# Decoder layer on one core: weights loaded in halves on two queues, chunk 1's query and key projections ahead of chunk 0's transposes

## Time and profile before

| | |
|---|---|
| median of three runs (lowest to highest) | 863.43 us (862.97 to 863.92) |
| the profiled execution, its span | 862.34 us, 860.5 us |
| PE busy | 749.3 us (87%) |
| DVE busy | 544.0 us (63%) |
| ACT busy | 321.1 us (37%) |
| POOL busy | 129.4 us (15%) |
| granted clock of TensorE, mean | 0.936 |
| DMA, mean | 48 GB/s |

### The profile page before, as it was taken

One profiled execution on the slowest core, in us unless ns is written; L12 is line 12 of the kernel. 1 busy time (PEld: TensorE's weight loads), 2 busy tenths in 40 slices (PEclk: granted clock), 3 DMA queues, 4 the chain that ended last, 5 costly groups with the idle time before them and its releaser, 6 DMA issues.

```text
span 860.5 us, 12175 instructions
## 1 busy us (share of the span) xinstructions
PE 749.3 (87%) x4742; PEld 612.8 (71%) x4742; DVE 544.0 (63%) x1032; ACT 321.1 (37%) x559; POOL 129.4 (15%) x173
## 2 busy tenths in 40 slices
PE   4799988887998799525999999999999999899993
PEld 3688777766877587414888777886768877688882
DVE  3567578775667758769771847855578746542214
ACT  4232232225422432157443335353443544341312
POOL 0452334023322233044000000000000000000000
PEclk9899999997998899655999999999999999999997
DMA  8400100013100130040102012002111030010201
GB/s 306 171 26 1 38 13 13 1 26 123 32 7 1 38 99 1 1 147 1 50 1 74 0 50 98 1 25 98 48 53 45 0 122 1 1 50 0 98 1 49
DMA packets 25356, 41.11 MB, mean 48 GB/s; under 512 B 4954, under 2 KB 7642, under 8 KB 25178
## 3 DMA queue, kind: packets, MB, share of 16 engines
q1 hardware_dynamic: 23194, 37.27, 12.9%
q10 hardware_dynamic: 2112, 3.15, 1.1%
HBM read 28.88 MB, written 11.53 MB: 47 GB/s over the span
## 4 chain that ended last, share of the span: by engine, by line
PE 39%; DVE 8%; ACT 2%; issue 2%; DVEq 0%; ACTq 0%
PE ps L1460 24%; PE ps L1470 11%; PE ps L457 2%; DVE act_s L279 2%; PE ps L468 2%; DVE act_s L376 1%; DVE silu L1393 1%; ACT silu L1330 1%; PE ps L477 1%; DVE xc L1406 1%; ACT h_hi L1313 1%; DVE xb L406 1%; DVE e_stats L409 1%; PE ps L450 1%; DVE w L279 0%
## 5 line engine op out<-in xcount | busy, mean ns | idle before, releaser
L1460 PE MATMUL ps<-x2T_lo,wgu_hi 128*128 128x512 f32 x352 | 141.1, 401 | 0.8 <-DVE x2T_lo L1383 0.8
L1460 PE MATMUL ps<-x2T_hi,wgu_lo 128*128 128x512 f32 x352 | 137.3, 390 | 0.0
L1460 PE MATMUL ps<-x2T_hi,wgu_hi 128*128 128x512 f32 x352 | 137.2, 390 | 0.0
L1393 DVE TENSOR_TENSOR silu<-ps,silu 128x512 f32<-128x512 f32 x44 | 30.4, 690 | 100.2 <-PE ps L1460 99.9
L1045 PE MATMUL ps<-wqkv_lo,xT_hi 128*128 128x512 f32 x192 | 83.0, 433 | 10.5 <-DVE masked L972 6.2
L1045 PE MATMUL ps<-wqkv_hi,xT_lo 128*128 128x512 f32 x192 | 78.4, 408 | 0.0
L1045 PE MATMUL ps<-wqkv_hi,xT_hi 128*128 128x512 f32 x192 | 78.2, 407 | 0.0
L1460 PEld LDWEIGHTS ps<-x2T_lo,wgu_hi 128*128 128x128 f32 x352 | 66.2, 188 | 15.3 <-DVE x2T_lo L1383 1.5
L1460 PEld LDWEIGHTS ps<-x2T_hi,wgu_lo 128*128 128x128 f32 x352 | 66.1, 188 | 14.0
L1460 PEld LDWEIGHTS ps<-x2T_hi,wgu_hi 128*128 128x128 f32 x352 | 66.2, 188 | 12.9
L1470 PE MATMUL ps<-wdn_lo,h_hi 128*128 128x512 f32 x176 | 70.6, 401 | 3.7 <-DVE h_lo L1377 3.7
(11 more groups left out here) (170 smaller groups left out, 1473.8 us busy)
## 6 DMA issues: line engine op xcount, KB each, us to landing
x_in<-in_x_dram SPq DMA_DIRECT2D x16, 256.0 KB, 3.5
w<-in_fside_BxS2xS_dram SPq DMA_DIRECT2D x4, 1024.0 KB, 6.5
x_dram<-xb SPq DMA_DIRECT2D x4, 1024.0 KB, 5.1
xc<-x_dram SPq DMA_DIRECT2D x4, 1024.0 KB, 5.4
xb<-x_dram SPq DMA_DIRECT2D x3, 1024.0 KB, 5.4
out_dram<-xc SPq DMA_DIRECT2D x3, 1024.0 KB, 4.2
z<-in_x_dram SPq DMA_DIRECT2D x3, 768.0 KB, 4.7
x_dram<-z SPq DMA_DIRECT2D x3, 768.0 KB, 4.0
```

The source lines that it names most:

```text
L1393: nc.vector.tensor_tensor(silu[:, it % 2, :], ps[5][:, :], silu[:, it % 2, :], ALU.mult)\
L1460: last = nc.tensor.matmul(dst[:, :], lhs, rhs, start=(k == 0 and n == 0), stop=(k == NK - 1 and n == 2))
```

## The change

The loads of Wq, Wk and Wv are each cut in two halves of 512 KB, the first on SyncE's queue, the second on ScalarE's, with a semaphore for each half. The identity matrix and x of chunk 1 move to ScalarE's queue; the tables, the mask and the scales follow in another order on SyncE's. On TensorE the transposes of x1 stand between q0 and k0; behind v0 come q1, the scale matmuls and k1, and then chunk 0's transposes. `weight_hi(3)` moves in ScalarE's list behind the copies of q1 and k1, and TensorE's waits for the scale columns and for Wo move to just ahead of the first y. `x_hi(1)` and `x_lo(1)` move ahead of Wv's rounding. In chunks 1 to 14 nothing changes.

```diff
@@ -537,9 +537,12 @@
 
 def attention_order():
 
-    yield from (("xT", 0), ("q", 0), ("k", 0), ("xT", 1), ("v", 0))
+    yield from (("xT", 0), ("q", 0), ("xT", 1), ("k", 0), ("v", 0), ("q", 1), ("k", 1))
     for n in range(CHUNKS):
-        yield from (("qT", n), ("kT", n), ("q", n + 1), ("k", n + 1), ("s0", n), ("s1", n), ("s2", n), ("s3", n))
+        yield from (("qT", n), ("kT", n))
+        if n > 0:
+            yield from (("q", n + 1), ("k", n + 1))
+        yield from (("s0", n), ("s1", n), ("s2", n), ("s3", n))
         if n % NC < NC - 1:
             yield ("kv", n)
         yield from (("v", n + 1), ("attn", n), ("xT", n + 2), ("y", n), ("ss", n))
@@ -613,7 +616,7 @@
         scale_rows = sq_halves[:, 0:2 * P].rearrange("p (m n) -> p m n", m=2)
         ident16 = sq_halves[:, 2 * P:3 * P]
 
-        tab_in, mask_in, wqkv_in, wo_in = (sem("tab_in"), sem("mask_in"), [sem(f"w{n}_in") for n in "qkv"],
+        tab_in, mask_in, wqkv_in, wo_in = (sem("tab_in"), sem("mask_in"), [[sem(f"w{n}_in_{m}") for m in range(2)] for n in "qkv"],
                                            sem("wo_in"))
         x_loaded = [sem("x_even_loaded"), sem("x_odd_loaded")]
         z_first_loaded, z_loaded = sem("z_first_loaded"), sem("z_loaded")
@@ -673,6 +676,11 @@
             for name, place in EXPERT0_STEPS.items():
                 if place == (n, part) and name in steps:
                     steps[name](0)
+
+        def load_half(eng, n, weight, half):
+
+            ks = slice(half * KH, (half + 1) * KH)
+            eng.dma_start(raw[:, n, ks], weight.rearrange("(k p) n -> p k n", p=P)[:, ks]).then_inc(wqkv_in[n][half], 16)
 
         gu_words = a["L0_ffn_gate_up_packed"].rearrange("(t p) w -> p t w", p=P).bitcast(U16)
         dn_words = a["L0_ffn_down_packed"].rearrange("(t p) w -> p t w", p=P).bitcast(U16)
@@ -723,15 +731,14 @@
                     sp.dma_start(dst, src).then_inc(words_in, 16)
 
             load_x(0)
-            sp.dma_start(ident_ones[:, :, :], table[:, 0:2 * P].rearrange("p (m n) -> p m n", m=2))\
-                .then_inc(ident_in, 16)
-            sp.dma_start(raw[:, 1], w_k.rearrange("(k p) n -> p k n", p=P)).then_inc(wqkv_in[1], 16)
+            load_half(sp, 0, w_q, 0)
+            load_half(sp, 1, w_k, 0)
+            sp.dma_start(tab[:, :], table[:, 2 * P:TABLE_W]).then_inc(tab_in, 16)
+            load_half(sp, 2, w_v, 0)
+            sp.dma_start(mask[:, :, :, :], masks.rearrange("p (j g c) -> p j g c", j=HG, g=NG)).then_inc(mask_in, 16)
             gu_rows, dn_rows = scale_rows[0:SCALES[0], 0, :], scale_rows[0:SCALES[1], 1, :]
             sp.dma_start(gu_rows, a["L0_ffn_gate_up_scales"].rearrange("g (t p) -> (g t) p", p=P)).then_inc(scales_in, 16)
             sp.dma_start(dn_rows, a["L0_ffn_down_scales"].rearrange("g (t p) -> (g t) p", p=P)).then_inc(scales_in, 16)
-            sp.dma_start(tab[:, :], table[:, 2 * P:TABLE_W]).then_inc(tab_in, 16)
-            load_x(1)
-            sp.dma_start(mask[:, :, :, :], masks.rearrange("p (j g c) -> p j g c", j=HG, g=NG)).then_inc(mask_in, 16)
             load_words(0)
             sp.wait_ge(w_ready, 4 * NK)
             load_z(0, True)
@@ -765,8 +772,12 @@
         @block.scalar
         def _(act):
             steps = expert.scalar_steps(act)
-            act.dma_start(raw[:, 0], w_q.rearrange("(k p) n -> p k n", p=P)).then_inc(wqkv_in[0], 16)
-            act.dma_start(raw[:, 2], w_v.rearrange("(k p) n -> p k n", p=P)).then_inc(wqkv_in[2], 16)
+            act.dma_start(ident_ones[:, :, :], table[:, 0:2 * P].rearrange("p (m n) -> p m n", m=2))\
+                .then_inc(ident_in, 16)
+            load_half(act, 0, w_q, 1)
+            load_half(act, 1, w_k, 1)
+            act.dma_start(x_in[:, 1, :], x_v[0][:, 1, :]).then_inc(x_loaded[1], 16)
+            load_half(act, 2, w_v, 1)
             act.dma_start(raw[:, 3], w_o.rearrange("(k p) n -> p k n", p=P)).then_inc(wo_in, 16)
             act.dma_start(rms_col[:, :], rms_w.rearrange("(k p) -> p k", p=P), allow_slow_non_contiguous=True)\
                 .then_inc(wo_in, 16)
@@ -774,7 +785,7 @@
             def weight_hi(n):
                 for k in range(NK):
                     if n < 3:
-                        act.wait_ge(wqkv_in[n], 16)
+                        act.wait_ge(wqkv_in[n][k // KH], 16)
                     else:
                         act.wait_ge(wo_scaled, k + 1)
                     dst = wqkv_hi[:, n, k, :] if n < 3 else wo_hi[:, k, :]
@@ -803,13 +814,17 @@
 
             def chunk(n):
                 b, c = divmod(n, NC)
+                if n == 0:
+                    projected(1, 0)
+                    projected(1, 1)
+                    weight_hi(3)
                 wait_full(act, "kT", n)
                 nc.scalar.activation(kT_hi[:, :, :], in_groups("kT", n), ACT.Copy).then_inc(kT_hi_done, 1)
                 wait_full(act, "qT", n)
                 nc.scalar.activation(qT_hi[:, :, :], in_groups("qT", n), ACT.Copy).then_inc(qT_hi_done, 1)
                 if c == 0 and b > 0:
                     ln_root_of(b - 1)
-                if n + 1 < CHUNKS:
+                if 0 < n < CHUNKS - 1:
                     projected(n + 1, 0)
                     projected(n + 1, 1)
                 beside(steps, n, 0)
@@ -833,11 +848,10 @@
             weight_hi(0)
             weight_hi(1)
             projected(0, 0)
+            x_hi(1)
             weight_hi(2)
             projected(0, 1)
-            x_hi(1)
             projected(0, 2)
-            weight_hi(3)
             act.wait_ge(ident_in, 16)
             nc.scalar.activation(ident16, ident, ACT.Copy).then_inc(ident16_set, 1)
             act.wait_ge(scale_ps, 2)
@@ -996,8 +1010,8 @@
             x_lo(0)
             weight_lo(0)
             weight_lo(1)
+            x_lo(1)
             weight_lo(2)
-            x_lo(1)
             dve.wait_ge(wo_in, 32)
             for k in range(NK):
                 nc.vector.tensor_scalar(raw[:, 3, k, :], raw[:, 3, k, :], rms_col[:, k:k + 1], None,
@@ -1047,8 +1061,21 @@
                 if ks[-1] == NK - 1:
                     last.then_inc(full[BANK_OF[u]], 1)
 
+            def scale_columns():
+                pe.wait_ge(ident16_set, 1)
+                pe.wait_ge(scales_in, 32)
+                at = 0
+                for m, n in enumerate(SCALES):
+                    nc.tensor.matmul(ps[6][:, at:at + n], scale_rows[0:n, m, :], ident16[0:n, 0:n],
+                                     start=True, stop=True).then_inc(scale_ps, 1)
+                    at += n
+
             def chunk(n):
                 c = n % NC
+                if n == 0:
+                    project(1, 0)
+                    scale_columns()
+                    project(1, 1)
                 pe.wait_ge(rot_done, 2 * (n + 1))
                 for p, u in enumerate(("qT", "kT")):
                     filled = start_use(u, n)
@@ -1103,6 +1130,9 @@
                     project(n + 1, 2, range(NK // 2, NK))
                 if n + 2 < CHUNKS:
                     transpose_x(n + 2)
+                if n == 0:
+                    pe.wait_ge(cols_set, 1)
+                    pe.wait_ge(w_ready, 4 * NK)
                 pe.wait_ge(o_lo_done, n + 1)
                 filled = start_use("y", n)
                 for k in range(NK):
@@ -1122,17 +1152,8 @@
             for p in range(3):
                 pe.wait_ge(w_ready, (p + 1) * NK)
                 project(0, p)
-                if p == 1:
+                if p == 0:
                     transpose_x(1)
-            pe.wait_ge(ident16_set, 1)
-            pe.wait_ge(scales_in, 32)
-            at = 0
-            for m, n in enumerate(SCALES):
-                nc.tensor.matmul(ps[6][:, at:at + n], scale_rows[0:n, m, :], ident16[0:n, 0:n],
-                                 start=True, stop=True).then_inc(scale_ps, 1)
-                at += n
-            pe.wait_ge(cols_set, 1)
-            pe.wait_ge(w_ready, 4 * NK)
             for n in range(CHUNKS):
                 chunk(n)
 
```

## The result

The changed kernel takes 867.14 us (median of 7, 865.45 to 868.25) against 863.92 (861.89 to 864.71) of the kernel before, run beside it: ratio 1.0036, 95% interval 1.0025 to 1.0046. It is slower by 3.2 us. The profiled execution has a span of 863.7 against 860.5.

The account below looks back on a forecast made before the run. TensorE's exit from the first 50 us was taken to bound the kernel, a shift there arriving nearly whole. Late x2 +1.5 and slow clock +1.7 gave +3.2 on the median 863.43: 866.6 us, range 862.6 to 868.5.

Parts of the forecast that it names:

- rival A: Chunk 0: x2 late, but the clock holds or a later fall vanishes in exchange; +0.5 to +2.2, 864.9 us; chance 0.2.
- Loads, q0, k0, v0, q1, k1: Front before chunk 0's transposes: q0 starts at 10.8 instead of 12.58, v0 at 20.0 instead of 21.16, k1 done at 28.5.
- rival C: Front loads: Wq's halves land no earlier than 9.29, q0 starts at 12.6 as now; +5.0, 868.4 us; chance 0.08.
- the bound I had named: q0 on TensorE: in the bounding case all of it runs slow, taking 0.4 us more.
- Wo's rounding: ScalarE, then VectorE: rounding starts at 29.1 instead of 24.72, subtraction takes 3.4, Wo ready at 33.2 (bounds 32.2 and 33.9).
- Chunk 0, "I charge 1.2": Scores to v1's first half at 1.2 GHz until about 39, partly covered by the masks' 3.0 us; cost 1.2 us.
- x2's load: SyncE: lands 12.8 us after Wo is ready, so x2's transposes start at 46.0 instead of 44.50, +1.5 (+0.5 to +2.2).
- Clock after the stall, +1.7: After 3.6 us idle before x2's transposes, y0, chunk 1's transposes and part of q2 run at 1.2 GHz; +1.7 us.
- The granted clock of one half between 45 and 51: TensorE around x2's transposes: a stretch at half clock there was named as a sign that the forecast is right.
- Passing through: From 50 us to the kernel's end: a shift at 50 us should arrive nearly whole at the end.
- Rival D: Past 100 us: VectorE-bound chunks take up the shift at 50 us; 863.4 to 864.5 us; chance 0.11.
- Rival B: Chunk 0: Wo's rounding not late, x2 in time, early scores count in full; -2.1, 861.3 us; chance 0.09.

Follow-up runs that it names:

- e8: Changed kernel with 24 idle-filling matmuls ahead of chunk 0's scores and x of chunk 2 loaded before SyncE's wait for Wo; ratio to the kernel before 0.9970.
- e7: Changed kernel with 24 idle-filling matmuls on TensorE between chunk 0's transposes and its scores; ratio to the kernel before 1.0043.
- e1: Changed kernel with x of chunk 2 loaded before SyncE's wait for Wo; ratio to the kernel before 1.0029.
- e11: Kernel before with 13 useless matmuls on TensorE just ahead of x2's transposes in chunk 0; ratio to the kernel before 1.0040.
- e2: Changed kernel with Wo rounded on ScalarE right behind the copy of v0 and the small identity; ratio to the kernel before 0.9975.
- e12: Changed kernel with Wo rounded behind v0's copy, chunk 2's x loaded before the wait for Wo, k1 back behind chunk 0's transposes; 855.44 us, ratio 0.9914.
- e10: Changed kernel with Wo rounded behind v0's copy, ten filling matmuls ahead of chunk 0's scores, chunk 2's x loaded before the wait for Wo; ratio 0.9948.
- e3: Changed kernel with Wo rounded behind v0's copy and x of chunk 2 loaded before the wait for Wo; ratio to the kernel before 0.9995.

## Why the prediction was right, and where its sum was not

The time (+3.2 forecast, +3.2 measured), its sign and the root of the loss, Wo's late rounding, were right. That the size agrees to a tenth is luck: two terms missed in opposite directions. x2's transposes came 2.83 later, not 1.5 and beyond the bound of 2.2; the clock after the wait cost nothing, not 1.7. In kind this is my rival A (x2 late, the clock holds), with a later x2 than I gave it. The 1.7 itself was half of a stretch of 3.3, where the row that I took it from gives 3.6.

- *Loads, q0, k0, v0, q1, k1.* q0 10.39 (forecast 10.8), v0 20.38 (20.0), chunk 0's transposes 29.14 (28.5). I had the rounding begin when Wq lands, at 7.5. It began at 7.10, straight behind x_hi(0) at 6.61, as before the change at 9.29 behind x_hi(0) at 8.80: there TensorE's first transposes had waited for the identity until 7.64. After, x_hi(0) follows a table load of ScalarE (5.31 to 6.59), and this its seven DMA issues, three more than before, which I had costed at nothing. The first half of Wq had landed at 1.18 + 5.5 = 6.7. So q0's gain came through the identity, and rival C, which hangs q0 on Wq's landing, misses this wait; what the halves alone gave, no run shows. All of q0 ran at 1.2 GHz, the bound I had named.
- *Wo's rounding.* Right in kind: ScalarE starts it at 29.83 (29.1). The subtraction was mis-sized: 4.25 instead of 3.4, above even the 3.71 of the row it was taken from, in which GpSimd worked beside it only part of the way. Wo ready at 34.7 (33.2, upper bound 33.9), scores at 36.14 (34.5).
- *Chunk 0, "I charge 1.2".* This term failed. From scores to TensorE ready for x2 takes 46.15 - 36.14 = 10.0 after, 6.7 in e8 with the clock held: 3.3 us. I had the clock return 4.4 us after work resumed, as in the rows of before; it took 7.4 (36.14 to 43.6). And the step "so part of it is covered" was wrong: the scores, which stand ahead of the masks, slow down too, and the slow first half of v1 ends at 43.5, later than the masks (41.4). Alone it cost nothing on the path, since x2 landed only at 47.3 (e7); it decides once x2 is early (x2's transposes at 46.10 in e1, at 41.80 in e8, whose front is 1.2 sooner).
- *x2's load.* 47.33 - 34.73 = 12.6 after Wo ready, forecast 12.8. x2 is what TensorE waits for, at 47.3 instead of 46.0; but TensorE came later too, so the wait was 1.18, not 3.6.
- *Clock after the stall, +1.7.* It did not happen: the clock held over the wait of 1.18. e7, where the wait was 3.19, shows that mechanism with its fall at 44.5 and return at 48. The granted clock of one half between 45 and 51, which I had named as a sign of being right, is not there in the changed kernel.
- *Passing through.* Right: 2.88 at chunk 1, 2.98 at chunk 8, 3.2 in the span, and e11. In 12 of the 13 kernels set against the one before, the spans differ by what chunk 8 did, to within 0.5 us (e8: 1.3). Rival D is out. Rival B's condition (Wo ready by 31.7) is what e2 made true, and it gave the gain.
- The Trainium skill (TensorE: Matmul & The Clock Gate, Part 1) has the release of the clock fall elsewhere from run to run. Here the runs agree, with one execution of each kernel: over the ten kernels with the changed loads and x1's transposes ahead of k0, v0 starts 8.8 us (e8: 19.29 - 10.53) to 10.2 us (e12: 20.48 - 10.32) behind q0, with the same work between.

What stays open: why the clock fell behind chunk 4 in some kernels and not in others. The single profiled executions move against the kernel before by up to 4.4 us between chunks 4 and 8 (e1: from +1.6 to +6.0), and no run fixed it. So the whole times, other than chunk 1, also hold this part, and they rank the kernels less surely than the front does.

## What to carry to other kernels

When work is moved ahead in one engine's list, look at what the other engines' lists put behind it: here two projections moved forward on TensorE pushed Wo's rounding behind their copies on ScalarE, and a semaphore that gated 3 MB of loads with it. Price idle time of TensorE with the slow stretch that follows it, and fill it with real work rather than shorten it. Remove coupled waits together, since one alone may show little.

## What the runs showed of the hardware

- The clock fell over an idle time of 2.27 us (e2) and held over one of 2.45 at 209 us (before). At 115.5, before, it fell right behind one of 1.94. The slow stretch in e2 lasted 6.8 us (32.0 to 38.8), the one in the changed kernel, with 5.96 us of idle time, 10.2 (33.3 to 43.6), and the one in e7, over the wait of 3.19, 3.4 (44.5 to 47.9).
- VectorE's subtraction of two SBUF operands took 4.25 us beside GpSimd's products and 2.50 without; GpSimd's four products took 4.11 beside it, and 2.76 in e2, where VectorE's work beside them had an operand in PSUM (kT_lo and qT_lo, 0.69 and 0.68, for 1.3 us of it):

```profile
29.51 2.76 POOL L876 TENSOR_TENSOR rot<-qkv,tab 128x256 f32<-128x256 f32 x4 [3.95 <-ACT qkv L801]
```

- The identity of 128 KB landed 3.3 us after its issue at the head of ScalarE's queue, and TensorE's first transposes began at 4.09 instead of 7.64.
- e10's ten times fall in two groups, 855.8 to 857.5 and 861.6 to 862.3, with one program. e3's twelve range from 856.0 to 868.7. The start of chunk 0's transposes differs between the kernels with the same work ahead of it too, from 27.96 (e7) to 29.28 (e1).
